# Output products that take tokens as weights in a test-time-training loop, and causal attention without its masked diagonal blocks

## The chip, the cores and the metric

The kernel runs on one core of a Trainium2 chip. The time is device microseconds of that core from start to end of one launch; a lower time is better. The times shown are medians of several executions, and beside them stands one execution that the hardware profiler recorded.

## The reference

Two transformer layers, each an attention-like part and a feed-forward part with adaptive layer norms, on a batch of 4 sequences of 512 tokens, 256 channels, in f32. The two parts that the change touches are the attention-like parts.

Layer 0 is a linear attention with fast weights. For each chunk of 64 tokens, with q, k, v per head (2 heads of 128 channels) and states w0, w1, w2 (128x128):

```python
gate = ki @ w0_; hb = ki @ w2_; hidden = silu(gate) * hb          # forward of keys
dhidden = vi @ w1_.transpose(0, 2, 1)                             # backward
w1g = newtonschulz5(einsum('bch,bcd->bhd', hidden * lr1i, vi))    # and w0g, w2g alike
w1_ = w1_ + w1g                                                   # then scaled to its first norm
o = (silu(qi @ w0_) * (qi @ w2_)) @ w1_                           # queries, then an RMS norm
```

Layer 1 is causal attention with 16 heads, 4 key groups, a latent of 64 channels for keys and values, and rotary positions on 64 channels. A query sees keys up to its own place, so in the last 128x128 square of each tile of queries the upper triangle is masked.

## The kernel before, in words

Everything is resident in SBUF; PSUM is eight banks of 128x512 f32. Each of the five engines runs its own program (TensorE, VectorE, ScalarE, GpSimd, and SyncE for the DMAs), in order, and they meet by counting semaphores. The order of the work is written out by hand.

**The loop over chunks** (`stage_fast_weights`). Eight steps (`NCH` = 8), each for all four sequences: a pair index `i` in 0 and 1, a half `j` of the partitions (64 tokens each), and a head `hd`, so eight (i, hd, j). Step 0 is written out, steps 1 to 5 are a hardware loop, steps 6 and 7 are written out, then comes `finish`. There are Q = 6 weight matrices of four units each: `3 * j + m`, m = 0, 1, 2 for w0, w2, w1. `state` holds them as they are updated and `weight` their transposes, which TensorE makes (`turn_weight`) and ScalarE or VectorE copies (`take_weight`).

A step on TensorE: `early_out` (the first of four calls of `out_product`, for the queries of the chunk before), `gates` (keys and values against the weights), two weight transposes, the second `out_product`, three groups of `gradient`, then `G_ORDER` (transposes GT of the gradients, column sums for their norms, and the third `out_product`, which stands there as `(OUT_ROWS, 0)`), then `INNER`, the Newton-Schulz products A, AA, Y, A1, AA1, YT, X2 for six matrices in a staggered order. Between these stand pieces of other work: the fourth `out_product` as `(OUT_ROWS, 1)`, `out_rows` (hidden against w1), `turn_out`, `project_out`, the turning of q, k, v of the next chunk, and `project_v` and `project_qk` of the one after it. At the step's end come `project_qk`, and four `turn_weight` as VectorE scales the states.

`out_product(m, j)` takes the weight as the stationary operand (128x128) and 64 tokens of `qT` as the moving one. Its result is transposed, channels on partitions: ScalarE takes the silu of bank 6 (`silu_out`, 128x512), and VectorE multiplies it with the other product (`hidden_out`, 128x512, after the third of the six A copies).

ScalarE, in a step: silu of q and k of the next chunk, weight copies, four activations for each pair of `gates`, gradient copies, `load_table(Sqrt)` and the root of the gradient norms (`g_norm`), copies of GT, AA, A1, YT, then the squares of states 4 and 5 (`SQUARED`), the roots of the weight norms (`root_state(1)`, then `root_state(0)` when VectorE's sums are there), `load_table(Silu)`, `take_proj`, weight copies 3 and 4. VectorE: squares of q and k, `backward`, squares of the gradients, the scaled copies (`scaled`), polynomials, updates of the state, `reduce_state` for states 3, 2, 0, 1, then `factors` and `scale_state`. GpSimd applies learning rates, moves q (`move_q`) and adds the output.

**The attention** (`stage_rest`). A batch is a tile of 128 queries of one row b of x: `ORDER` = (1, 3, 0, 2), 16 batches, with widths of 256, 512, 128 and 384 keys. A slot `t` is a batch and a pair of heads p (8 pairs): TensorE `score`, VectorE `largest` (the mask is added and the maximum taken in one instruction), ScalarE `exponential`, VectorE `invert`, GpSimd `normalize`, VectorE `turn` (transposes 32x32 blocks). `weigh(n - 1)` stands in slot 2 of batch n, all in one piece (the last batch has it in four pieces behind its slots). It multiplies blocks of 32 keys, in tiles of 32 rows by 64 columns: row group i holds queries 32i to 32i + 31, e is the head of the pair, and the moving operand is 8 pairs x 32 queries = 256 columns. `take_out` copies the result, `project_out` projects it. In the other slots stand the query projections of the next batch (`project_q`, "rope" in slots 0 and 1, "latent" in 4 and 5), and the values, keys and norms of the next row b. The feed-forward part of layer 0 lies between loop and attention, the routing and the experts of layer 1 behind them.

## Time and profile before

| what | value |
| --- | --- |
| median of three executions | 1028.23 us (1025.88 to 1028.37) |
| the profiled execution, its own time | 1024.87 us |
| span of the profile, first to last instruction | 1023.1 us |
| granted clock of TensorE over the span | 0.998 |
| busy: TensorE, VectorE, ScalarE, GpSimd | 970.8, 700.8, 564.5, 435.2 us |
| the loop, steps 1 to 7 | about 87 us to 360 us |
| the feed-forward part | about 362 us to 603 us |
| the attention's slots | 603 us to about 975 us |

Times in the profile are microseconds from its first instruction. PE is TensorE, PEld its weight loads, DVE is VectorE, ACT is ScalarE, POOL is GpSimd, SP is SyncE. Matmuls are pipelined and overlap, and a matmul's recorded duration is mostly latency: what a group costs is seen in the start of the next group. A f32 matmul has two records, a transpose one.

### The profile page before, as it was taken

How to read it: one execution, taken by the hardware profiler on the slowest of the kernel's cores; microseconds unless marked ns; L12 is line 12 of the kernel's file. 1: busy time of each engine (PE TensorE's matmuls, PEld its weight loads, DVE VectorE, ACT ScalarE, POOL GpSimd, SP SyncE). 2: the span in 40 equal slices, each digit the busy share in tenths (PEclk: the TensorE clock that was granted, in tenths of full speed). 3: DMA queues.
4: the chain of work that ended last, by engine and by line, in shares of the span. 5: the costliest groups of instructions: out<-in, count | busy, mean ns of one | idle time of the engine just before them, and what ended most of it. 6: DMA issues, size and time to landing. Idle time of an engine off the chain costs nothing.

```text
span 1023.1 us, 25038 instructions
## 1 busy us (share of the span) xinstructions
PE 970.8 (95%) x9714; PEld 738.6 (72%) x9714; DVE 700.8 (69%) x2121; ACT 564.5 (55%) x1450; POOL 435.2 (43%) x391
## 2 busy tenths in 40 slices
PE   5888999999999999999999999999999999999988
PEld 3566897888887755675656769786878687868646
DVE  4889988988989952213222676866787678766884
ACT  3668778777788742222223465565565556555541
POOL 1221140340542711101002666775677567779720
PEclk9999999999999999999999999999999999999999
DMA  9250000000000001900002321322132222211202
GB/s 313 70 196 2 2 0 0 0 0 0 0 2 2 1 1 36 322 1 0 1 1 53 83 62 44 72 59 57 43 74 53 58 48 66 60 42 44 93 3 84
DMA packets 32812, 52.36 MB, mean 51 GB/s; under 512 B 7760, under 2 KB 17744, under 8 KB 31824
## 3 DMA queue, kind: packets, MB, share of 16 engines
q1 hardware_dynamic: 32720, 51.10, 18.2%
q8 instruction: 62, 1.02, 0.4%
q14 instruction: 30, 0.25, 0.1%
HBM read 21.98 MB, written 2.10 MB: 24 GB/s over the span
## 4 chain that ended last, share of the span: by engine, by line
PE 53%; DVE 4%; ACT 2%; issue 1%
PE quad L2105 12%; PE quad L2064 10%; PE quad L1705 8%; PE quad L2122 7%; PE quad L2008 5%; PE quad L2136 5%; PE quad L2200 1%; PE quad L2072 1%; PE quad L1591 1%; ACT act_probs L2359 1%; ACT act_probs L2368 1%; PE quad L2027 1%; DVE act_probs L2460 1%; DVE wq_wo L2474 1%; DVE x_pairs L2490 0%
## 5 line engine op out<-in xcount | busy, mean ns | idle before, releaser
L2711 POOL TENSOR_TENSOR act_probs<-act_probs,rden 128x512 f32<-128x512 f32 (+3 forms) x128 | 169.1, 1327 | 110.6 <-DVE rden L2479 110.6
L2359 ACT ACTIVATE act_probs<-act_probs,neg_max 128x256 f32<-128x256 f32 (+3 forms) x256 | 141.0, 553 | 81.6 <-DVE neg_max L2460 81.4
L2064 PEld LDWEIGHTS quad<-hT,ug_queries 128*128 128x128 f32 x1024 | 122.6, 192 | 14.1 <-issue 7.7
L2064 PE MATMUL quad<-hT,ug_queries 128*128 128x128 f32 x1024 | 124.7, 275 | 0.8 <-DVE act_probs L1720 0.5
L2460 DVE CUSTOM_DVE_ANT_0 act_probs<-quad,mask 128x256 f32<-128x256 f32 (+3 forms) x256 | 115.0, 485 | 0.4 <-issue 0.3
L1705 PE MATMUL quad<-hT,ug_raw_switch 128*128 128x512 f32 x256 | 113.9, 595 | 0.0
L1720 DVE SCALAR_TENSOR_TENSOR act_probs<-quad,ws_up,silu_keys 128x512 f32<-128x512 f32 x32 | 24.0, 750 | 97.1 <-ACT silu_keys L1715 97.1
L1715 ACT ACTIVATE silu_keys<-quad,ws_gate 128x512 f32<-128x512 f32 x32 | 22.0, 688 | 118.6 <-PE quad L1705 118.6
L1705 PEld LDWEIGHTS quad<-hT,ug_raw_switch 128*128 128x128 f32 x256 | 47.4, 190 | 55.1 <-issue 54.3
L2479 DVE RECIPROCAL rden<-den 128x2 f32<-128x2 f32 x128 | 20.3, 159 | 94.6 <-ACT act_probs L2359 94.3
L2105 PE MATMUL quad<-down_raw_out,ug_raw_switch 128*128 128x256 f32 (+3 forms) x256 | 79.6, 438 | 3.2 <-DVE neg_max L2460 3.1
L2105 PE MATMUL quad<-silu_keys,ug_raw_switch 128*128 128x256 f32 (+3 forms) x256 | 79.7, 439 | 2.8 <-DVE neg_max L2460 2.0
L2474 DVE STREAM_TRANSPOSE wq_wo<-act_probs 128x1024 f32<-128x1024 f32 (+1 forms) x64 | 70.7, 1106 | 0.7 <-POOL act_probs L2711 0.4
L1426 POOL TENSOR_TENSOR hidden<-gate_silu,hb 128x256 f32<-128x256 f32 x16 | 12.0, 753 | 124.2 <-ACT hb L969 124.2
L2136 PE MATMUL quad<-down_keys,act_probs 128*128 128x256 f32 x256 | 60.5, 380 | 0.8 <-ACT act_probs L2368 0.8
L2105 PEld LDWEIGHTS quad<-down_raw_out,ug_raw_switch 128*128 128x128 f32 x256 | 42.4, 190 | 24.5 <-issue 15.2
L2105 PEld LDWEIGHTS quad<-silu_keys,ug_raw_switch 128*128 128x128 f32 x256 | 42.0, 190 | 24.9 <-issue 13.3
L2008 PE MATMUL quad<-down_raw_out,act_probs 128*128 128x256 f32 x256 | 56.1, 379 | 2.0 <-PEq L1510 2.0
L2136 PEld LDWEIGHTS quad<-down_keys,act_probs 128*128 128x128 f32 x256 | 47.9, 190 | 12.2 <-issue 2.9
L2008 PEld LDWEIGHTS quad<-down_raw_out,act_probs 128*128 128x128 f32 x256 | 48.3, 190 | 9.6 <-issue 3.3
L2122 PE MATMUL quad<-wq_wo,latent_rows 32*64 32x256 f32 x1792 | 51.5, 376 | 1.6 <-ACT gate L2345 0.8
L1206 DVE SCALAR_TENSOR_TENSOR q_bf<-quad,silu_keys 128x512 bf16<-128x512 f32 x72 | 46.3, 684 | 5.2 <-PE quad L645 5.0
(330 smaller groups left out, 2286.5 us busy)
## 6 DMA issues: line engine op xcount, KB each, us to landing
rope_swapped<-gate SPq DMA_DIRECT2D x120, 64.0 KB, 2.0
ug_raw_switch<-gate SPq DMA_DIRECT2D x60, 128.0 KB, 2.3
ug_raw_switch<-in_wmod SPq DMA_DIRECT2D x4, 512.0 KB, 7.1
x_pairs<-in_x SPq DMA_DIRECT2D x4, 512.0 KB, 7.6
x_rows<-x_pairs SPq DMA_DIRECT2D x8, 256.0 KB, 5.0
wq_wo<-in_wq_nopeT SPq DMA_DIRECT2D x1, 2048.0 KB, 8.5
wq_wo<-in_wo SPq DMA_DIRECT2D x1, 2048.0 KB, 13.0
ug_queries<-in_switch_w SPq DMA_DIRECT2D x1, 2048.0 KB, 7.7
```

Of the source, the lines that this page charges most:

```text
L1206: nc.vector.scalar_tensor_tensor(q_bf[:, q, :], bank[q][:], ca_b2, a_bf[:, q, :], ALU.mult, ALU.add).then_inc(taken[q], 1)
L1705: mm = k.nc.tensor.matmul(k.bank[2 * (m % 2) + w][:], self.w_ug[:, w, kt, P * m:P * m + P], k.hT[:, kt, 2 * i:2 * i + 2, 4 * C * u:4 * C * ...
L1720: k.nc.vector.scalar_tensor_tensor(self.act_t[:, m, :], k.bank[2 * (m % 2)][:], k.ws_up[:, m:m + 1], self.silu[:, m % 2, :], ALU.mult, ALU ...
L2008: mm = nc.tensor.matmul(bank[4 + q // 2][:, D * (q % 2):D * (q % 2) + D], act_t[:, m, P * q:P * q + P], w_down[:, ffn.place(m), :], start= ...
L2064: mm = nc.tensor.matmul(out[:, P * i:P * i + P], w[:, kt, HP * half + i, :], k.hT[:, kt, b, cols], start=(kt == 0), stop=(kt == KT - 1))
L2105: nc.tensor.matmul(score_bank[t % AHEAD][e][:, 0:width(n)], query[:, n % 2, e, p, :], keys[b % 2][:, p // 2, 0:width(n)], start=True, stop ...
L2122: mm = nc.tensor.matmul(av[LORA * e:LORA * e + LORA, i, :], val[rows, b % 2, j, :], src[rows, j, e, :, :], start=(j == 0), stop=(j == bloc ...
L2136: mm = nc.tensor.matmul(out[:, 0:D], oT[:, p, :], w_vo[:, p, :], start=(p == 0), stop=(p == NP - 1))
L2359: nc.scalar.activation(tile, tile, ACT.Exp, bias=neg_max[:, r, e:e + 1], scale=-1.0, accum_out=den[:, r, e:e + 1])\
L2460: nc.vector.tensor_tensor_reduce(probs[:, t % RING, e, 0:cols], score_bank[t % AHEAD][e][:, 0:cols], mask[:, L - cols:L], -QK_SCALE, 3e38, ...
L2474: nc.vector.transpose(turned_of[batches[n][1]][:, :, :, p, :].rearrange("p j e c -> p e j c"), probs[:, t % RING, :, 0:width(n)].rearrange ...
L2711: nc.gpsimd.tensor_tensor(tile, tile, rden[:, t % RING, :].unsqueeze(2).to_broadcast([P, 2, cols]), ALU.mult)\
```

## The change

The loop: `out_product` is used in `finish` alone. In its place `out_gate(t, i)` takes the tokens of q as the stationary operand (64 columns, on the column half j of the array) and both weights w0 and w2 as the moving one (256 columns), as `gates` does for k. Silu and product are done in halves (`silu_gate`, `hidden_rows`), tokens on partitions; then `turn_hidden` transposes the result with four f32 transposes, and ScalarE copies it (`take_hidden`). `early_out` goes; `gates` waits for the scaled states only ahead of its second part. At the step's end the second half of `project_qk` stands behind the last two `turn_weight`. State 3 is squared on ScalarE instead of VectorE from step 1 on (`SQUARED`), `take_proj` stands between the two roots, and the squares of q and k of the second pair stand at VectorE's start of the step. In step 7 GpSimd waits for a norm ahead of `move_q`.

The attention: for odd pairs p the queries of a tile are in reverse order, by a backward view of the moving operand in `project_q`. So in block d of the last four, row group i needs its even pairs only where d <= i and its odd pairs only where d <= 3 - i; `weigh` leaves the others out (`DIAGONAL`). The order in a block is row group outside (0, 3, 1, 2), head e inside. The mask and the rope tables have a backward half, `take_out` has an instruction for each parity and puts the order right.

Buffers: gate_pairs, hadamard and ws_dp share one tensor, in which the cosine table comes to lie after the loop; the cosine and sine tables are 512 KB each instead of 256, the mask has five squares instead of four.

In the diff below the table `TAKEN`, the buffers, `finish`, the rope tables and renamed semaphores are left out; context lines are dropped. `TAKEN` gets `(TURN_HID, 0)` ahead of `(AA, 0)`, for `take_hidden`; `out_rows` waits for it.

```diff
@@ -418,24 +419,24 @@
-    SQUARED = (4, 5)
+    SQUARED, SQUARED_FIRST = (4, 5, 3), (4, 5)
-    PROJECT_V, TURN_OUT, TURN_V, TURN_QK, OUT_ROWS, SUMS, START = range(PH, PH + 7)
-    G_ORDER = ((GT, 0), (SUMS, 0), (OUT_ROWS, 0), (SUMS, 1), (SUMS, 2), (GT, 2), (SUMS, 3), (SUMS, 4), (GT, 4), (SUMS, 5))
+    PROJECT_V, TURN_OUT, TURN_V, TURN_QK, OUT_ROWS, SUMS, START, OUT_GATE, TURN_HID = range(PH, PH + 9)
+    G_ORDER = ((GT, 0), (SUMS, 0), (OUT_GATE, 1), (SUMS, 1), (SUMS, 2), (GT, 2), (SUMS, 3), (SUMS, 4), (GT, 4), (SUMS, 5))
-    INNER = ((A, 0), (A, 1), (OUT_ROWS, 1), (START, 0), (A, 2), (A, 3), (AA, 0), (A, 4), (AA, 1), (START, 1), (A, 5), (TURN_V, 0), (AA, 2), (OUT_ROWS, 0), (START, 2), (AA, 3), (Y, 0), (AA, 4), (AA, 5), (START, 3), (TURN_QK, 0), (Y, 1),
+    INNER = ((A, 0), (A, 1), (TURN_HID, 0), (START, 0), (A, 2), (A, 3), (AA, 0), (A, 4), (AA, 1), (START, 1), (A, 5), (TURN_V, 0), (AA, 2), (OUT_ROWS, 0), (START, 2), (AA, 3), (Y, 0), (AA, 4), (AA, 5), (START, 3), (TURN_QK, 0), (Y, 1),
-    NORM_QK, HIDDEN, MEAN_OUT, NORM_OUT = 1, 2, 0, 0
+    NORM_QK, MEAN_OUT, NORM_OUT = 1, 0, 0
...
@@ -560,12 +561,33 @@
+                    if i == 0 and (isinstance(t, bass.RuntimeValue) or t > 0):
+                        pe.wait_ge(s["w_scaled"], Q * t)
+            def out_gate(t, i):
+                if i == 0:
+                    pe.wait_ge(s["proj_taken"], t)
+                    pe.wait_ge(s["q_moved"], t)
+                else:
+                    pe.wait_ge(s["out_hidden"], 2 * t - 1)
+                for hd in range(H):
+                    for j in range(2):
+                        mm = nc.tensor.matmul(bank[6][C * j:C * j + C, 2 * HD * hd:2 * HD * hd + 2 * HD],
+                                              qT[:, i, hd, C * j:C * j + C], weight[:, 3 * j:3 * j + 2, H * i + hd, :],
+                                              start=True, stop=True)
+                mm.then_inc(s["out_summed"], 1)
+            def turn_hidden(t):
+                pe.wait_ge(s["out_hidden"], 2 * t)
+                for u in range(U):
+                    mm = nc.tensor.transpose(bank[6][:, P * u:P * u + P], h_o[:, P * u:P * u + P], k.eye[:])
+                mm.then_inc(s["o_turned"], 1)
...
@@ -577,7 +599,10 @@
-                pe.wait_ge(s["out_hidden"], c + 1)
+                if at == 6:
+                    pe.wait_ge(s["hid_taken"], c + 1)
+                else:
+                    pe.wait_ge(s["out_hidden"], 2 * NCH - 1)
...
@@ -647,8 +666,6 @@
-                if not first:
-                    early_out(t)
                 pe.wait_ge(s["qkv_taken"], 3 * (t + 1))
...
@@ -656,7 +673,6 @@
                         begin(q, G)
-                    pe.wait_ge(s["w_scaled"], Q * t)
                 gates(t)
...
@@ -668,8 +684,7 @@
                     turn_weight(t - 1, 2)
-                    begin(0, G)
-                    out_product(0, 0, 0)
+                    out_gate(t, 0)
...
@@ -714,9 +729,7 @@
                     else:
-                        if n == 0:
-                            pe.wait_ge(s["out_silued"], t)
-                        out_product(1, n)
+                        out_gate(t, n)
                 pe.wait_ge(s["g_columns_taken"], t + 1)
...
@@ -741,11 +754,10 @@
+                    elif ph == TURN_HID and not first:
+                        turn_hidden(t)
-                        if n == 1:
-                            out_product(1, 1)
-                        else:
-                            out_rows(t - 1)
+                        out_rows(t - 1)
...
@@ -795,10 +807,10 @@
+                    turn_weight(t, 0)
+                    turn_weight(t, 1)
-                    turn_weight(t, 0)
-                    turn_weight(t, 1)
...
@@ -915,6 +927,15 @@
+            def silu_gate(t, i):
+                act.wait_ge(s["out_summed"], 2 * (t - 1) + i + 1)
+                nc.scalar.activation(h_o[:, H * P * i:H * P * i + H * P].rearrange("p (h d) -> p h d", h=H),
+                                     bank[6][:].rearrange("p (h g d) -> p h g d", h=H, g=2)[:, :, 0, :], ACT.Silu).then_inc(s["out_silued"], 1)
+            def take_hidden(t):
+                act.wait_ge(s["o_turned"], 2 * t - 1)
+                nc.scalar.activation(hid_o[:].rearrange("p i h c -> p (i h c)"), bank[6][:], ACT.Copy).then_inc(s["hid_taken"], 1)
...
@@ -979,10 +999,12 @@
-                    silu_out(t - 1)
+                    silu_gate(t, 0)
+                if not first:
+                    silu_gate(t, 1)
...
@@ -1040,22 +1064,23 @@
-                        act.wait_ge(s["w_squared"], 2 * t + 2)
-                    act.wait_ge(s["w_reduced"], 4 * t + 4 - 3 * j)
+                        act.wait_ge(s["w_squared"], 3 * t + 2)
+                    if first or j == 0:
+                        act.wait_ge(s["w_reduced"], 1 if j == 1 else 3 * t + 4)
-                for q in SQUARED:
+                for q in SQUARED_FIRST if first else SQUARED:
+                if first:
+                    nc.scalar.activation(add[:, 0, 0:1], k.neg_half[:, 0:1], ACT.Copy).then_inc(s["proj_taken"], 1)
+                else:
+                    take_proj(t - 1)
-                if first:
-                    nc.scalar.activation(add[:, 0, 0:1], k.neg_half[:, 0:1], ACT.Copy).then_inc(s["proj_taken"], 1)
-                else:
-                    take_proj(t - 1)
...
@@ -1128,8 +1153,14 @@
-            def hidden_out(c, at=6):
-                dve.wait_ge(s["out_silued"], c + 1)
+            def hidden_rows(t, i):
+                dve.wait_ge(s["out_silued"], 2 * (t - 1) + i + 1)
+                to = h_o[:, H * P * i:H * P * i + H * P].rearrange("p (h d) -> p h d", h=H)
+                nc.vector.tensor_tensor(to, bank[6][:].rearrange("p (h g d) -> p h g d", h=H, g=2)[:, :, 1, :], to, ALU.mult)\
+                    .then_inc(s["out_hidden"], 1)
+            def hidden_out(c, at):
+                dve.wait_ge(s["out_silued"], 2 * NCH - 1)
...
@@ -1177,6 +1208,8 @@
+                if not first:
+                    hidden_rows(t, 0)
...
@@ -1209,6 +1242,8 @@
+                    dve.wait_ge(s["qkv_acted"], 3 * (t + 1) + 2)
+                    square_qk(t + 1, 1, (0, 1, 2, 3))
...
@@ -1228,12 +1263,13 @@
-                if more:
-                    dve.wait_ge(s["qkv_acted"], 3 * (t + 1) + 2)
-                    square_qk(t + 1, 1, (0, 1, 2, 3))
-                    if first:
-                        mods.guard_gates(dve, 0)
-                else:
+                if not first:
+                    hidden_rows(t, 1)
+                if first:
+                    dve.wait_ge(s["qkv_acted"], 5)
+                    square_qk(1, 1, (0, 1, 2, 3))
+                    mods.guard_gates(dve, 0)
+                elif not more:
...
@@ -1251,8 +1287,6 @@
-                    if not first and n == HIDDEN:
-                        hidden_out(t - 1)
...
@@ -1305,7 +1339,7 @@
-                    if n == 3:
+                    if first and n == 3:
...
@@ -1433,6 +1467,7 @@
+                    pool.wait_ge(norms.xn_done, norms.groups[LN0B].end)
...
@@ -1835,6 +1870,10 @@
+    EVERY, FORWARD, BACKWARD = slice(0, NP), slice(0, NP, 2), slice(1, NP, 2)
+    DIAGONAL = [[(i, EVERY if d <= min(i, ROWS - 1 - i) else FORWARD if d <= i else BACKWARD)
+                 for i in (0, 3, 1, 2) if d <= max(i, ROWS - 1 - i)] for d in range(ROWS)]
+    LAST_OF = [max(i, ROWS - 1 - i) for i in range(ROWS)]
...
@@ -1961,6 +2000,13 @@
+    def in_order(tokens, p):
+        return tokens[:, ::-1] if p % 2 else tokens
+    def mask_of(n, p):
+        q = batches[n][1]
+        return mask[:, q::-1, :] if p % 2 else mask[:, QT - q:QT + 1, :]
...
@@ -2061,7 +2107,7 @@
-                        mm = nc.tensor.matmul(out[:, P * i:P * i + P], w[:, kt, HP * half + i, :], k.hT[:, kt, b, cols],
+                        mm = nc.tensor.matmul(out[:, P * i:P * i + P], w[:, kt, HP * half + i, :], in_order(k.hT[:, kt, b, cols], i),
...
@@ -2116,11 +2162,13 @@
-                    for e in range(2):
-                        for i in range(ROWS):
-                            rows = slice(BLK * i, BLK * i + BLK)
-                            mm = nc.tensor.matmul(av[LORA * e:LORA * e + LORA, i, :], val[rows, b % 2, j, :], src[rows, j, e, :, :],
-                                                  start=(j == 0), stop=(j == blocks - 1))
+                    d = max(0, j - (blocks - ROWS))
+                    for i, pairs in DIAGONAL[d]:
+                        rows = slice(BLK * i, BLK * i + BLK)
+                        for e in range(2):
+                            out = av[LORA * e:LORA * e + LORA, i, :].rearrange("p (n c) -> p n c", c=BLK)
+                            mm = nc.tensor.matmul(out[:, pairs, :], val[rows, b % 2, j, :], src[rows, j, e, pairs, :],
+                                                  start=(j == 0), stop=(d == LAST_OF[i]))
...
@@ -2364,8 +2412,9 @@
-                for heads in [slice(0, NP)] if n < NB - 1 else [slice(0, HP), slice(HP, NP)]:
-                    nc.scalar.activation(to[:, heads], src[:, heads], ACT.Copy).then_inc(s["oT_taken"], 1)
+                for lo, hi in [(0, NP)] if n < NB - 1 else [(0, HP), (HP, NP)]:
+                    nc.scalar.activation(to[:, lo:hi:2], src[:, lo:hi:2], ACT.Copy)
+                    nc.scalar.activation(to[:, lo + 1:hi:2, ::-1, ::-1], src[:, lo + 1:hi:2], ACT.Copy).then_inc(s["oT_taken"], 1)
...
@@ -2457,8 +2506,9 @@
-                    nc.vector.tensor_tensor_reduce(probs[:, t % RING, e, 0:cols], score_bank[t % AHEAD][e][:, 0:cols],
-                                                   mask[:, L - cols:L], -QK_SCALE, 3e38, ALU.add, ALU.min,
+                    nc.vector.tensor_tensor_reduce(probs[:, t % RING, e, 0:cols].rearrange("p (w c) -> p w c", c=P),
+                                                   score_bank[t % AHEAD][e][:, 0:cols].rearrange("p (w c) -> p w c", c=P),
+                                                   mask_of(*divmod(t, NP)), -QK_SCALE, 3e38, ALU.add, ALU.min,
```

## Rows read from the trace of the kernel before

**Rows 1.** The page: busy time by engine, and the chain that ended last.
```profile
PE 970.8 (95%) x9714; PEld 738.6 (72%) x9714; DVE 700.8 (69%) x2121; ACT 564.5 (55%) x1450; POOL 435.2 (43%) x391
...
PE 53%; DVE 4%; ACT 2%; issue 1%
```

**Rows 2.** One loop step by windows: its length, busy time per engine, clock.
```profile
166.26:205.50 39.24, 38.52 (x472) 32.92 (x471) 35.34 (x115) 30.79 (x83) 10.57 (x14) 1.00 0.00 0
```

**Rows 3.** TensorE's timeline in that step: start, length, operation, records.
```profile
166.26 1.08 PE L559 MATMUL quad<-weight,kT 128*64 128x256 f32 x8
167.17 0.61 PE L565 MATMUL quad<-state,vT 128*64 128x128 f32 x8
...
178.25 1.06 PE L574 MATMUL quad<-qT,weight 128*128 128x64 f32 x8
179.14 0.61 PE L645 MATMUL quad<-act_probs 128*128 128x128 bf16 x8
...
191.85 0.61 PE L592 MATMUL quad<-eye,o_n 128*128 128x128 f32 x4
192.30 0.39 PE L645 MATMUL quad<-silu_keys 128*128 128x128 bf16 x4
...
201.52 1.26 PE L618 MATMUL quad<-eye,state 128*128 128x128 f32 x8
202.62 1.02 PE L537 MATMUL quad<-w_qkv,h_chunk 128*128 128x512 f32 x2
203.48 1.04 PE L618 MATMUL quad<-eye,state 128*128 128x128 f32 x8
204.45 1.10 PE L574 MATMUL quad<-qT,weight 128*128 128x64 f32 x8
205.50 1.08 PE L559 MATMUL quad<-weight,kT 128*64 128x256 f32 x8
```

**Rows 4.** ScalarE's timeline at the end of that step.
```profile
200.43 0.21 ACT L1045 ACTIVATE w_n<-w_rows 128x12 f32<-128x12 f32 x1 [2.07 <-DVE w_rows L1287]
...
202.54 1.08 ACT L937 ACTIVATE weight<-quad 128x512 f32<-128x512 f32 x2
```

**Rows 5.** VectorE's timeline in that step.
```profile
167.92 0.43 DVE L1158 TENSOR_TENSOR d_hb<-quad,gate_silu 128x256 f32<-128x256 f32 x1 [1.36 <-PE quad L565]
...
180.17 0.68 DVE L1134 TENSOR_TENSOR out_hidden<-quad,out_silu 128x512 f32<-128x512 f32 x1
...
200.78 1.29 DVE L1303 TENSOR_TENSOR state<-state,w_f 128x512 f32<-128x512 f32 x2
...
202.45 2.50 DVE L1303 TENSOR_TENSOR state<-state,w_f 128x512 f32<-128x512 f32 x4
```

**Rows 6.** Groups by line, 60 to 300 us: count | busy us, mean ns.
```profile
L1287 DVE CUSTOM_DVE_ANT_0 act_probs<-state 128x128 f32<-128x128 f32 x96 | 21.3, 288 | 0.0
...
L1036 ACT ACTIVATE act_probs<-state 128x128 f32<-128x128 f32 x48 | 14.0, 297 | 0.0
```

**Rows 7.** TensorE's timeline in the attention, batches 2 and 3.
```profile
626.01 7.17 PE L2122 MATMUL quad<-wq_wo,latent_rows 32*64 32x256 f32 x256 [0.29 <-issue]
633.10 1.16 PE L2105 MATMUL quad<-silu_keys,ug_raw_switch 128*128 128x128 f32 x8
...
664.97 1.10 PE L2105 MATMUL quad<-down_raw_out,ug_raw_switch 128*128 128x256 f32 x4 [0.88 <-DVE neg_max L2460]
```

**Rows 8.** VectorE's timeline ahead of that wait.
```profile
662.59 1.75 DVE L2490 TENSOR_TENSOR x_pairs<-x_pairs,rope_sin 128x512 f32<-128x512 f32 x1
```

**Rows 9.** Groups by line, whole span, TensorE.
```profile
L2064 PE MATMUL quad<-hT,ug_queries 128*128 128x128 f32 x1024 | 124.7, 275 | 0.8 <-DVE act_probs L1720 0.5
...
L2159 PE MATMUL quad<-hT,ug_raw_switch 32*32 32x384 f32 x128 | 4.5, 493 | 1.4 <-DVE attn_gated L2500 1.0 <-DVE ug_raw_switch L2554 0.3
...
L2170 PE MATMUL quad<-hT,ug_raw_switch 32*32 32x128 f32 x128 | 2.5, 277 | 0.9 <-issue 0.9
```

59 lines of the change are left out of this document (31 added, 28 removed).

## The prediction

> **What bounds the kernel now.** I read the page first, then the waits and the timelines of one loop step, then those of the attention. TensorE is busy for 95% of the span, and most of the chain that ended last is its own work [rows 1]; in the loop its granted clock is 1.00, the 2.4 GHz level [rows 2]. So a step is worth what it takes from TensorE's stream, if no other engine is late instead.
>
> The first place of the change is the loop over the eight chunks. A step lasts 39.24 us, TensorE busy for 38.52, VectorE for 35.34 and ScalarE for 30.79 [rows 2]. The reader should use the start times in TensorE's timeline, not the durations, since matmuls overlap: a group costs the distance to the next group's start. One f32 matmul shows as two records. A call of `out_product` (eight records, 128x128 weights, 64 moving columns) costs 0.89 us (178.25 to 179.14) among the A products, and 1.05 us at the step's start with the wait behind it (204.45 to 205.50). The same number of records with 64 columns of weights and 256 moving columns costs 0.91 us (166.26 to 167.17), though each moves four times the columns [rows 3]. So the former cost is not that of its columns. Four f32 transposes cost 0.45 us (191.85 to 192.30) [rows 3].
>
> The second place is the weighing of the values in the attention, in 32x64 tiles: 16 key blocks take 7.09 us, 626.01 to 633.10 [rows 7], so 0.443 us for a block of sixteen records, or 27.7 ns a record. TensorE is there bound by its own stream too, but not everywhere: at 664.97 it has waited 0.88 us for VectorE [rows 7], which is at work on the keys of the next batch, 1.75 us in one instruction [rows 8].
>
> **The loop, part by part.** (1) Four calls of `out_product` go, and two of `out_gate` come, each built like one half of `gates`: 0.91 us each. Two of them stand where `out_product` stood (ahead of the gradients, and in `G_ORDER`), so some 0.9 becomes 0.91 twice; I count nothing. The other two places lose their product: 1.05 at the step's start and 0.89 among the A products. `turn_hidden` adds 0.45. TensorE's stream is 1.05 + 0.89 - 0.45 = 1.49 us shorter per step.
>
> (2) What replaces the cover at the step's start. The early product hid ScalarE's copies of weights 0 and 1. Now the second part of `project_qk`, 0.86 us (202.62 to 203.48, [rows 3]), moves behind the last two transposes and covers them. Those transposes can now come earlier than VectorE's scaled state 0: VectorE scales two states from 200.78 and four from 202.45 [rows 5], and the transposes of weight 3 start at 201.52 [rows 3]. VectorE itself comes earlier, because `reduce_state(3)` leaves it: four squares at 21.3/96 = 0.22 us [rows 6], 0.9 us. The last updates then wait for TensorE's last products instead, so perhaps 0.4 of the 0.9 are gained beyond the shift of the whole step. That is enough for weight 3, while weight 0 is a little late: I leave 0.15 us for a new wait there.
>
> (3) ScalarE gets state 3, four squares at 14.0/48 = 0.29 us [rows 6], their reads overlapping: 1.2 us more. It had idled 2.07 us before the second root [rows 4], and VectorE needs that root only after its own remaining three reductions. `take_proj` moves into that idle time as well, which pulls the first weight copy (202.54, [rows 4]) some 0.5 us forward. I count nothing here, the idle time being longer than the squares; the upper bound is that the third square gives 0.8 us per step back.
>
> (4) The hidden product in halves. VectorE has one product over 512 columns, 0.68 us at 180.17, in the middle of its scaled copies [rows 5]. It becomes two over 256, about 0.43 each (as the row at 167.92, [rows 5]): one in idle time behind `backward`, one behind the column sums. The A copies are thus 0.6 us closer together, which matches the product that TensorE loses there, so that TensorE's gain can be realised. ScalarE's half `silu_gate` now stands ahead of the table load for the root of the gradient norms; it delays that root by 0.15 us, of which VectorE feels 0.05, as its squares behind the column sums go. Queued behind that root are the root of the q and k norms and the five copies of GT, for which the A products wait. Its `take_hidden` lies behind the last GT copy, where ScalarE waits for TensorE anyway.
>
> (5) The squares of q and k for the second pair move to the step's start, 0.84 us, ahead of `backward`. VectorE waits there 1.36 us for `gates` [rows 5]: they fit, with 0.05 us to spare. Both bounds: nothing, or 0.4 us per step if the second silu comes late, since the whole backward pass is queued behind them.
>
> Sum: 1.49 - 0.15 - 0.05 = 1.29 us a step. Seven steps (1 to 7) have the products: 9.0 us. Bounds: 7 x 1.49 = 10.4, and 7 x (1.29 - 0.8) = 3.4.
>
> **The attention.** (6) Of the last four key blocks of each tile of queries, the masked parts go. Odd head pairs hold their tokens backward, so every row group streams 640 columns of 1024: 256, 256 or 128, 128, and 128 for two row groups alone. Four blocks take 4 x 0.443 = 1.77 us now, and at best 640/1024 of that, 1.11: a saving of 0.66. Issue is strictly in order, and a short tile waits behind a long one at two places; that and the cost of short records take some back. 128 records of 384 columns in 32x32 tiles cost 4.5 us and of 128 columns 2.5 us: 35 and 20 ns [rows 9]. There sixteen tiles run side by side, here eight, so 128 columns less are worth the same 15 ns a record here, if no floor stands in the way, and the floor may be as high as those 20. I take 16 ns, between 27.7 - 15 and 20. Then 24 full records at 27.7, 24 short ones at 16 and the eight of the last block, which have half of the tiles, at 27 make 1.26 us: 0.5 us saved. Bounds 0.66, and 0.2 for the floor and a loss at each change of width.
>
> (7) That happens 16 times. At the third batch of each of the first three rows of x the gain ends in the wait for VectorE of [rows 7]; so it does at the very end, where VectorE's routing is the longer branch, and half of it in the last batch. 11.5 x 0.5 = 5.8 us; bounds 11.5 x 0.2 = 2.3 and 16 x 0.66 = 10.6.
>
> (8) Costed at nothing: `take_out` in two instructions instead of one (about 0.1 us of ScalarE, ahead of an output product four slots later; without that cover 0.1 us x 16); the mask and the rope tables as views of more dimensions (same element counts); tables of twice the size, which land while TensorE runs the feed-forward part; the shared buffer, whose first users are done by then. In step 7 GpSimd now waits for `normalize` of VectorE ahead of `move_q`; behind it stands only an `add_out`, and TensorE needs the moved q in `finish`, a projection and eight transposes later.
>
> (9) The one operation with no near row: half of the query projection now reads its moving operand backward. The rows have 1024 records of it, all forward, 124.7 us or 0.12 us each [rows 9]. Bounds: nothing, or a doubled stream for 512 records, 62 us. I take nothing, as the nearest row: 256 columns taken in two pieces far apart run at full rate in `gates` [rows 3]. 
>
> **Sum.** 9.0 + 5.8 = 14.8 us off the profiled execution of 1024.9 us: 1010.1. The median of the runs shown is 3.4 us above that execution, so 1013.5.
>
> **Rivals.**
> A (forecast), both parts gain: 1013.5, own range 1008 to 1019; chance 0.64.
> B, the loop gives most of it back. VectorE and ScalarE have more to do in the same stretches, and the second `silu` or the third square ends last. For it: VectorE's 35.34 of 39.24 us, and margins of 0.05. Against: its own work falls by 0.6. 3.4 + 5.8 = 9.2: 1019; chance 0.12.
> C, the attention gives nothing: short records cost as much as long ones, or VectorE and GpSimd, not TensorE, set the slots. For it: [rows 8]. Against: TensorE's stream is unbroken in most batches. 9.0: 1019; chance 0.12. B and C together: 1025; 0.03.
> D, slower: the backward read. It decides from 14.8 us / 512 = 29 ns a record, a quarter over today's distance. At the doubled rate 1013.5 + 62 = 1075; chance 0.06.
> E, slower: tiles in the same rows don't overlap. The order in a block becomes row group outside, column half inside. Where the second half had to wait for the first, the 96 whole blocks would go from 0.44 to 0.89 us and the 16 diagonals from 1.26 to 2.2: some 58 us more, 1071. `gates` speaks against it: its column halves share all rows, and 256 columns pass in 0.91/8 = 0.114 us [rows 3], no more than 128 columns in the query projection, which has the whole array (0.12, [rows 9]); so the halves do run side by side. The Trainium skill ("TensorE: Matmul & The Clock Gate", the mechanism of row and column tiling) says that a weight load overlaps with running matmuls only where the row group differs; by that rule E would hold, and by the row A does. Chance 0.03.
>
> **How the numbers follow.** A measurement here tells 0.3%, 3 us, from no change. Faster by more: A, B, C, and half of both together: 0.64 + 0.24 + 0.02 = 0.90, less 0.02 for runs that scatter by 2.5 us: 0.88. Same: 0.03. Slower: 0.09. The range reaches from A's low end to B and C: 1007 to 1021 holds some 0.82.
>
> **What would show it.** TensorE's timeline: no 64-column product at the start of a step, `gates` directly behind the 512-column projection, step length near 38 us; `out_gate` at 0.91 us. ScalarE's idle time before the second root gone, VectorE's 1.36 us before `backward` gone. In the attention: the four last blocks of a tile in 1.2 to 1.3 us, the query projection at 0.12 us a record in both directions, the stall of [rows 7] longer by about 0.5. I am wrong if a step stays over 38.5 us, if the projection's records lengthen, or if the waits for VectorE in the attention grow by as much as the weighing shrinks.

## The result and the profile after

The changed kernel takes 1016.8 us (median of 4 runs, 1013.95 to 1018.83), the kernel before 1027.1 in the runs beside it: a ratio of 0.9898, 95% interval 0.9876 to 0.9919. A later pairing gave 0.9896 (0.9879 to 0.9913). The forecast was 1013.5, range 1007 to 1021, faster.

The page of the changed kernel, busy times first, then the chain (compare [rows 1]):

```profile
PE 954.8 (94%) x9502; PEld 718.5 (71%) x9502; DVE 695.5 (69%) x2072; ACT 576.7 (57%) x1537; POOL 435.5 (43%) x391
...
PE 46%; DVE 8%; ACT 2%; issue 2%; POOL 1%; DMA 0%; SPq 0%; DVEq 0%; POOLq 0%
```

One loop step of it by windows, from the first `gates` record of step 3 to that of step 4, as in [rows 2] (columns: length, busy time of PE, PEld, DVE, ACT, POOL, granted clock, DMA share, GB/s):

```profile
166.75:205.05 38.30, 37.45 (x460) 30.60 (x459) 34.75 (x106) 32.36 (x92) 10.57 (x14) 1.00 0.00 0
```

The step has lost 0.94 us, not 1.29. TensorE's timeline of that step, the lines that answer to [rows 3]:

```profile
163.25 1.04 PE L643 MATMUL quad<-eye,state 128*128 128x128 f32 x8
164.70 1.26 PE L643 MATMUL quad<-eye,state 128*128 128x128 f32 x8 [0.41 <-DVE state L1337]
165.79 1.02 PE L538 MATMUL quad<-w_qkv,h_chunk 128*128 128x512 f32 x2
166.75 1.08 PE L560 MATMUL quad<-weight,kT 128*64 128x256 f32 x8
...
170.52 1.08 PE L581 MATMUL quad<-weight,qT 128*64 128x256 f32 x8
171.53 0.72 PE L632 MATMUL quad<-d_hb,k_lr 64*128 64x128 f32 x8
...
174.82 1.08 PE L581 MATMUL quad<-weight,qT 128*64 128x256 f32 x8
175.84 0.35 PE L720 MATMUL quad<-ones_bf,q_bf 128*128 128x1 bf16 x8
...
178.81 0.61 PE L589 MATMUL quad<-eye,out_silu 128*128 128x128 f32 x4
179.25 0.69 PE L664 MATMUL quad<-act_probs 128*128 128x128 bf16 x8
```

The reader is to see three things. `gates` (L560) stands directly behind the projection part (L538), as forecast. An `out_gate` (L581) costs 1.01 and 1.02 us to the next group's start, where 0.91 was forecast. The transposes of weight 0 (164.70) wait 0.41 us for VectorE, where 0.15 was.

In the attention, TensorE's timeline of the second weighing and of the wait in the third batch ([rows 7]), and the query projection by line ([rows 9]):

```profile
621.96 6.52 PE L2170 MATMUL quad<-wq_wo,latent_rows 32*64 32x256 f32 x248 [0.29 <-issue]
628.41 1.16 PE L2151 MATMUL quad<-silu_keys,ug_raw_switch 128*128 128x128 f32 x8
...
660.35 1.10 PE L2151 MATMUL quad<-down_raw_out,ug_raw_switch 128*128 128x256 f32 x4 [1.48 <-DVE neg_max L2509]
```

```profile
L2110 PE MATMUL quad<-hT,ug_queries 128*128 128x128 f32 x1024 | 124.7, 275 | 1.2 <-ACT act_probs L2417 0.5 <-DVE act_probs L1755 0.5
```

Sixteen key blocks take 6.45 us (621.96 to 628.41) instead of 7.09: 0.64 less, where 0.5 was forecast. The wait for VectorE has grown from 0.88 to 1.48 us: in that batch nearly all of the gain ends in it. The projection with half of its tokens backward costs the same 124.7 us.

**Where the time came from.** Milestones of TensorE, in us between first records (the start is counted from 0.13 us of the profile), in the profiled executions:

| stretch | before | changed | changed, second profile |
|---|---|---|---|
| start to gates(0) | 31.92 | 33.53 | 32.99 |
| steps 0 and 1 | 94.97 | 94.79 | 94.80 |
| steps 2 to 6 | 195.86 | 191.14 | 191.10 |
| step 7 to the feed-forward part | 35.27 | 36.21 | 36.20 |
| feed-forward part | 190.97 | 189.57 | 191.26 |
| to the first weighing | 54.71 | 55.04 | 55.06 |
| first to last weighing | 372.88 | 365.49 | 368.57 |
| last weighing to last product | 42.66 | 42.30 | 42.30 |

So the loop gives 4.0 us, nothing of it in steps 0 and 1, and 1.4 more at the head of the feed-forward part, where TensorE had waited for VectorE's last state; 5.4 in all where 9.0 were forecast. TensorE's timeline there, before and changed:

```profile
361.72 1.28 PE L618 MATMUL quad<-eye,state 128*128 128x128 f32 x8
363.43 0.63 PE L618 MATMUL quad<-eye,state 128*128 128x128 f32 x4 [0.44 <-issue]
365.07 0.66 PE L618 MATMUL quad<-eye,state 128*128 128x128 f32 x4 [1.01 <-DVE state L1303]
365.56 2.74 PE L1705 MATMUL quad<-hT,ug_raw_switch 128*128 128x512 f32 x6
```

```profile
359.23 1.04 PE L643 MATMUL quad<-eye,state 128*128 128x128 f32 x8
360.75 1.21 PE L643 MATMUL quad<-eye,state 128*128 128x128 f32 x8 [0.48 <-issue]
361.79 3.60 PE L1740 MATMUL quad<-hT,ug_raw_switch 128*128 128x512 f32 x8
```

VectorE's timeline shows why the last state was late: three of its last four scalings of a state before, and all four in the changed kernel.

```profile
362.64 4.06 DVE L1303 TENSOR_TENSOR state<-state,w_f 128x512 f32<-128x512 f32 x3
```

```profile
359.95 2.50 DVE L1337 TENSOR_TENSOR state<-state,w_f 128x512 f32<-128x512 f32 x4
```

Before, GpSimd runs its two instructions on the output from 362.91 and 364.54 us (1.54 and 1.61 us), and the two scalings beside them take 1.76 us each instead of 0.69. In the changed kernel GpSimd's two start at 356.19 and 358.02 us, end ahead of the last four scalings, and slow one of the first two. `attn_only` has the late meeting and `loop_only` hasn't. The nearest cause is `take_proj`, which now stands ahead of ScalarE's second root and so gives GpSimd its operand earlier; no run moves it alone.

The attention gives 7.4 + 0.4 where 5.8 were forecast. That makes 13.2 us; the start, 1.6 us later, and 0.3 ahead of the first weighing leave the 11.2 between the two spans. The second profile of the changed kernel loses 1.7 us in the feed-forward part and 3.1 in the attention to falls of the granted clock and waits that the first doesn't have (last section).

### The profile page after: what moved, and what is told of

It is laid out like the page before. It is cut to its first block, busy times and chain, and to the rows that moved or that the text cites. A ratio compares the mean times of both kernels' runs of the same rounds, so it can differ in the third digit from the quotient of the medians.

```text
span 1011.9 us, 24653 instructions
## 1 busy us (share of the span) xinstructions
PE 954.8 (94%) x9502; PEld 718.5 (71%) x9502; DVE 695.5 (69%) x2072; ACT 576.7 (57%) x1537; POOL 435.5 (43%) x391
## 4 chain that ended last, share of the span: by engine, by line
PE 46%; DVE 8%; ACT 2%; issue 2%; POOL 1%; DMA 0%; SPq 0%; DVEq 0%; POOLq 0%
PE quad L2151 9%; PE quad L1740 8%; PE quad L2110 8%; PE quad L2054 5%; PE quad L2170 5%; PE quad L2184 4%; DVE act_probs L2509 2%; DVE wq_wo L2524 2%; PE quad L2248 1%; DVE x_pairs L2541 1%; ACT act_probs L2407 1%; PE quad L2118 1%; PE quad L1626 1%; PE quad L2073 1%; ACT hT L1639 1%
## 5 line engine op out<-in xcount | busy, mean ns | idle before, releaser
L2110 PE MATMUL quad<-hT,ug_queries 128*128 128x128 f32 x1024 | 124.7, 275 | 1.2 <-ACT act_probs L2417 0.5
L2509 DVE CUSTOM_DVE_ANT_0 act_probs<-quad,mask 128x128 f32<-128x128 f32 (+3 forms) x160 | 65.3, 445 | 0.0
L2509 DVE CUSTOM_DVE_ANT_1 act_probs<-quad,mask 128x256 f32<-128x256 f32 (+2 forms) x96 | 49.4, 551 | 0.0
```

Source lines behind the costliest of these rows:

```text
L2110: mm = nc.tensor.matmul(out[:, P * i:P * i + P], w[:, kt, HP * half + i, :], in_order(k.hT[:, kt, b, cols], i), start=(kt == 0), stop=(kt ...
L2509: nc.vector.tensor_tensor_reduce(probs[:, t % RING, e, 0:cols].rearrange("p (w c) -> p w c", c=P), score_bank[t % AHEAD][e][:, 0:cols].rea ...
```

## The experiments

A step length in the trace repeats to 0.02 us between kernels with the same loop, a whole execution only to some us (the changed kernel's four lie between 1013.95 and 1018.83); so small edits are judged by the trace.

**One part alone.** `loop_only` leaves the attention as before, `attn_only` the loop.

> The loop's part of the change alone; the attention is as before. Theory, the two parts are independent: a steady step lasts 38.3 us as in the changed kernel (39.24 before), the feed-forward part ends some 3.8 us earlier than before, and the attention's weighings last as before (5.1 and 6.8 us for 12 and 16 key blocks). Time about 3 to 4 us under before, ratio 0.9965. Rival, the loop's gain of 0.94 us in a step reaches the end in full (6 x 0.94 = 5.6 us and more), and what was missing in the profile of the changed kernel (a start 1.6 us later, at a granted clock of 0.50 in 20 to 22 us) was an accident of that one execution: then the start is at 31.9 us here and the time 5 to 6 us under before.

> The attention's part of the change alone, with the reversed order of tokens of odd head pairs, and the shared buffer; the loop is as before. Theory, the parts are independent: step 39.24 us, each of 16 weighings 0.52 us shorter, first to last weighing 365.5 us as in the changed kernel (372.9 before), time about 7 us under before, ratio 0.993. Rival, with the loop as before the tables of twice the size land while nothing else changed, and the first batch waits for them: then the ratio is nearer 1 and the gap shows before the first weighing. The first steps of the program: the granted clock in 20 to 22 us is 1.00 if its fall in the changed kernel was an accident of one execution, 0.50 if the kernel brings it.

Measured: `loop_only` 1023.2 us, ratio 0.9964 (0.9949 to 0.9978); `attn_only` 1020.9, 0.9949 (0.9932 to 0.9965). The two ratios together make 8.9 us of gain, against 10.5 by the ratio of the whole change: the parts add up within the intervals. Steps 2 to 4 are 38.28 to 38.29 us in the first, 39.22 to 39.24 in the second; from first gates to feed-forward part 322.05 and 325.84 (326.11 before, 322.14 changed). The loop's gain up to there is 4 us, so the first theory holds; steps 0 and 1 give nothing (94.79 in the first, 94.72 in the second). The feed-forward part is 190.98 us in the second, as before, so its 1.4 us are the loop change's too. In `loop_only` a fall of the granted clock takes them back there (191.27). From its first to its last weighing it has 373.98 us, against 372.88 before; these two are why 5.4 us of the trace are 3.7 in the times, as far as one profile can tell. `attn_only` falls short of the 7 us expected: 5.2, with 366.75 us from first to last weighing instead of 365.5. Starts are at 33.22 and 33.15 us without a fall of the clock: the early start of the profile before (31.92) was no property of it (31.35 to 33.53 in all profiles).

**Nothing left out.** `reversed_whole`: the changed kernel, with

```
-    DIAGONAL = [[(i, EVERY if d <= min(i, ROWS - 1 - i) else FORWARD ...
-    LAST_OF = [max(i, ROWS - 1 - i) for i in range(ROWS)]
+    DIAGONAL = [[(i, EVERY) for i in (0, 3, 1, 2)] for d in range(ROWS)]
+    LAST_OF = [ROWS - 1] * ROWS
```

> The changed kernel, but every weighing goes over all key blocks of all pairs again, with the reversed tokens and with the new order of tiles (row group outside, column half inside); the masked parts add zeros. Theory, the backward read and the new order cost nothing and all of the attention's gain is the columns left out: weighings last 5.1 and 6.8 us as before, the query projection 0.12 us a record, time that of the loop change alone (7 us over the changed kernel). Rival, the new order has a part in the gain or in a loss: weighings of whole blocks differ from 0.443 us a block; 0.02 us a block would be 3 us in the time.

Measured: 1023.8 us, 0.9977 (0.9966 to 0.9988), beside 0.9964 for `loop_only`. From first to last record the weighings of 4, 8 and 12 blocks last 1.61, 3.34 and 5.07 us, as before. The four of 16 blocks spread from 6.86 to 8.25 (`loop_only`: 6.79 to 7.41). So backward reads and the new order of tiles are free as far as this can tell; what makes the weighings of 16 blocks scatter wasn't followed. Their two intervals overlap, and 1 us between them is not decided.

**Left out in the plain way.** `triangle`, on top of `loop_only`:

```
                 for j in range(lo, hi):
-                    for e in range(2):
-                        for i in range(ROWS):
+                    d = max(0, j - (blocks - ROWS))
+                    for i in range(d, ROWS):
+                        for e in range(2):
```

> The loop change, and an attention that leaves the masked parts out in the plain way: tokens forward for all pairs, and key block d of the last four goes only to the row groups from d on, 10 of 16 pairs of row group and block, each record at full width. Theory, what a weighing costs is the stream of its fullest row group: the last row group still streams all four blocks, so nothing is saved: weighings within 0.1 us of before, time that of the loop change alone. Rival, what it costs is records issued: 12 of 32 records of the last four blocks go, 27.7 ns each (0.443 us for 16): 12 x 0.0277 = 0.33 us less a weighing, 5 us less in all; if four blocks shrink by the share of records, 0.66 us, 10 us in all.

(A matmul here is two records, so the rival's price should have read 24 of 64 records: 0.66 us by either count.) Measured: 1021.9 us, 0.9954 (0.9941 to 0.9968). TensorE's timeline of the second weighing:

```profile
623.37 7.17 PE L2157 MATMUL quad<-wq_wo,latent_rows 32*64 32x256 f32 x232 [0.29 <-issue]
630.47 0.71 PE L2139 MATMUL quad<-silu_keys,ug_raw_switch 128*128 128x128 f32 x4
```

232 records instead of 256 take 7.10 us, as before. Shown: what a weighing costs is the stream of the row group with the most columns. It is not the number of records, and not the sum of the columns either, which is 640 of 1024 of the last four blocks both here and in the changed kernel. The reversal of odd pairs is what makes the omission pay, since it brings every row group to 640 of 1024 columns; and 1.77 x 384/1024 = 0.66 is what it paid (0.64).

**The third square on VectorE again**, and **the cover back** ahead of the transposes 0 and 1:

```
-    SQUARED, SQUARED_FIRST = (4, 5, 3), (4, 5)
+    SQUARED, SQUARED_FIRST = (4, 5), (4, 5)
...
-                    if first and n == 3:
+                    if n == 3:
                         reduce_state(3)
```

```
+                    if ahead:
+                        project_qk(t + 2, 1, [1])
                     turn_weight(t, 0)
                     turn_weight(t, 1)
-                    if ahead:
-                        project_qk(t + 2, 1, [1])
```

> The changed kernel with the squares of state 3 back on VectorE, behind the fourth update, in steps 1 to 7 too. Judged by the length of the steps of 38.30 us, from gates to gates. Theory, VectorE's chain of updates, sums, factors and scalings sets the end of the step now: the transposes of weight 0 already wait 0.41 us for its state 0, so its four sums, 0.9 us, come on top: 39.1 to 39.2 us, and that wait grows to about 1.3. The move of the squares is then what makes the loop's change a gain at all. Rival, the forecast's upper bound: the squares cost ScalarE as much as they give VectorE, and the step changes by less than 0.2 us either way.

> The changed kernel with the last part of the query and key projection (0.96 us) again ahead of the transposes of weights 0 and 1. Judged by the steps of 38.30 us. Theory: the wait of 0.41 us for state 0 goes, but the part no longer covers ScalarE's two copies of the weights, 0.6 us each, for which gates waits: steps 38.5 to 38.6 us. Rival, the wait for state 0 is a pure loss and the copies are early enough: steps 37.9 us.

Measured by steps 2 to 4: 38.68 to 38.69 and 38.35 to 38.36 us, against 38.30. Having VectorE's squares of state 3 on ScalarE is worth 0.39 us a step, not 0.9. TensorE's wait for state 0 didn't grow as expected (0.42 us); all of VectorE's end of the step comes later. In the changed kernel VectorE waits 0.24 us for TensorE ahead of its last update (158.66), so part of the 0.9 had gone into waiting there; the rest wasn't followed. It is worth 0.75 in step 6 (37.89 to 38.64), which has no projection to put ahead, and about 1.2 at the head of the feed-forward part (192.48 with a fall of the clock, 191.26 in the changed kernel with one). Moving the cover is worth nearly nothing (0.05). In `cover_back` the wait of 0.41 us for VectorE's state 0 is gone, and `gates` waits 0.79 us for ScalarE's copy of a weight instead.

**out_gate in the same shape of tiles.** `same_mode`:

```
                 gates(t)
+                if not first:
+                    out_gate(t, 0)
...
                     turn_weight(t - 1, 5)
                     turn_weight(t - 1, 2)
-                    out_gate(t, 0)
```

ScalarE's `silu_gate` and copy of weight 2 change places for it, and VectorE's copy of weight 5 comes later.

> The changed kernel with the first out_gate directly behind gates, whose tile shape it shares, and the transposes of weights 5 and 2 behind it; ScalarE and VectorE take those weights correspondingly later. Judged by the steps of 38.30 us. Theory, an out_gate costs 1.02 us and not the forecast's 0.91, and its neighbours up to 0.1 more, because TensorE drains where the shape of its tiles changes from 128x128 to 128x64 and back; one change to and one from it less are worth 0.15 to 0.2 us: 38.1 to 38.15. Rival, the 1.02 is the reading of qT or the wait for a bank, and the place is nothing: 38.3. Second rival, the later copies of weights 5 and 2 hold up the gradients: 38.5 or more.

Measured: 38.14 to 38.15 us, 0.15 less. From the first record of `gates` to that of the gradients it is 4.64 us instead of 4.78, with no wait in either, so the changes of tile shape (128 x 128 to 128 x 64 and back) around one `out_gate` are what is left to cost that. But steps 0 and 1 took 96.75 us together instead of 94.5 to 95.2 in the kernels with the changed loop and no fall of the clock there. Step 0, whose code is untouched, took 55.87 of them (54.2 to 55.4 in the others), at a granted clock of 0.80 and 0.78 in 50 to 54 and 54 to 58 us.

**Step 1.** VectorE's and TensorE's timelines of the changed kernel at the start of step 1:

```profile
86.99 0.19 DVE L395 TENSOR_SCALAR out_hidden<-out_hidden 128x72 f32<-128x72 f32 x1
...
89.65 0.49 DVE L1393 TENSOR_SCALAR w_proj<-w_proj,onorm 128x512 f32<-128x512 f32 x1
...
91.57 0.81 DVE L1136 CUSTOM_DVE_ANT_0 act_probs<-qkv 128x128 f32<-128x128 f32 x1
...
92.95 0.41 DVE L1189 TENSOR_TENSOR d_hb<-quad,gate_silu 128x256 f32<-128x256 f32 x1
```

```profile
92.02 1.08 PE L581 MATMUL quad<-weight,qT 128*64 128x256 f32 x8
94.94 1.16 PE L632 MATMUL quad<-d_hb,k_lr 64*128 64x128 f32 x16 [1.84 <-DVE d_gate_out L1191]
```

Here VectorE has 3.2 us of work on the learning rates and the projection's weights ahead of its step (86.99 to 90.19), and the idle time into which the squares were moved doesn't exist. The gradients wait 1.84 us (0.21 before). Two kernels, with VectorE's step 1 taken out of its loop:

```
late_in_step_1, in step 1 alone:     room_in_step_1, in step 1 alone:
 square_qk(t + 1, 0, ...)             backward(t, first)
-square_qk(t + 1, 1, ...)            +w_proj scaled, ffn.scale_signs(dve)
 backward(t, first)                   (both were ahead of step 1)
 ...
 hidden_rows(t, 1)
+square_qk(t + 1, 1, ...)
```

> The changed kernel with VectorE's squares of the second pair of q and k at their former place, behind the column sums, in step 1 alone. Judged by gates(1) to gates(2), 40.21 us in the changed kernel and 39.79 before. Theory: in step 1 VectorE comes late, with 3.2 us of work on the learning rates ahead of its step, so the squares moved ahead of the backward pass, 0.84 us and more, lie on the path, where TensorE's gradients wait 1.84 us for it (0.21 before): step 1 takes 38.8 to 39.3 us, and the wait falls under 0.9. Rival, the wait of 1.84 us is the backward pass itself on late weights: step 1 stays above 40 us.

> The changed kernel, with VectorE's scaling of the projection weights and of the signs (0.65 us) in step 1 behind the backward pass, where VectorE waits for TensorE's gradients anyway. Theory: VectorE's work between the scaling of the states and the backward pass is what the gradients of step 1 wait for; their wait of 1.84 us falls to about 1.2, and with work taken out of the path and not only moved along it, it stays gained: gates(0) to gates(2) 94.1 us, against 94.8. Rival: it is given back in the same step, and 94.5 us or more come out.

Measured: the wait fell to 1.43 and 1.57 us (it is 1.84 and 2.24 in the changed kernel's own two profiles), and steps 0 and 1 together took 94.50 and 94.55 us, against 94.79. Both theories fall in their size, and the numbers of both rivals came: step 1 of `late_in_step_1` stays above 40 us (40.34), and `room_in_step_1` is above 94.5. Of the later squares 0.3 us stay. TensorE's timeline of `late_in_step_1` shows one place where the rest went:

```profile
101.34 0.40 PE L664 MATMUL quad<-act_probs 128*128 128x128 bf16 x4 [0.61 <-ACT act_probs L972]
```

ScalarE's copies of GT stand behind `root_qk`, which waits for these squares. Of the 0.65 us moved out of the way 0.25 stay; what takes the rest was not followed.

**The changed kernel again, and three edits joined.** `best` is `same_mode` with the edit of `room_in_step_1`, and in step 7 two of `normalize`'s four instructions behind the fourth scaled copy of A. In step 7 VectorE does `normalize` (1.37 us) ahead of g_norm, which the later half product now delays. TensorE's timeline there in the changed kernel:

```profile
331.99 0.70 PE L664 MATMUL quad<-act_probs 128*128 128x128 bf16 x8
333.37 0.23 PE L664 MATMUL quad<-silu_keys 128*128 128x128 bf16 x1 [0.68 <-DVE silu_keys L1234]
```

> The changed kernel as it is, once more, beside the next one on the same chip, and for a second trace of it. Theory: the loop from the first gates to the first product of the feed-forward part lasts 322.1 us again, steps 38.30, since these repeated to 0.1 us in three other kernels with the same loop; the ratio to before is 0.989 to 0.991. The start, which was 31.4 to 33.5 us in ten profiles with no relation to the kernel, and the feed-forward part (189.6 to 192.5) may differ by 1 to 2 us. Rival: the fall of the granted clock to 0.50 at 20 to 22 us belongs to the changed kernel; then it comes again, and the start is 33.5.

> The changed kernel with three edits: the first out_gate directly behind gates (0.15 us a step); in step 1 VectorE's scaling of the projection weights and of the signs behind the backward pass instead of ahead of the step (0.65 us); in step 7 two of the four normalizations behind the fourth scaled copy of A, so that g_norm is not kept waiting (0.3 to 0.7 us, the wait of 0.68 of TensorE). Theory: loop from first gates to the feed-forward part 320.0 to 320.6 us, against 322.1, and a time 1.5 to 2 us below the changed kernel's on the same chip. Rival: VectorE is late again at the next place in each of the two steps (as in step 1 with the later squares, where 0.42 us gained were lost 5 us on), so that only the 6 x 0.15 us stay: 321.2.

Measured: the changed kernel 1016.85 us, with the loop as expected (322.09) and no fall of the clock at the start, so that one belongs to an execution and not to the kernel. `best` 1017.6 us, 0.9912 (0.9896 to 0.9929): not better. Step 7 did gain 1.0 us up to the feed-forward part (35.19), and then TensorE waited 2.66 us. VectorE's, TensorE's and GpSimd's timelines in `best`, and windows:

```profile
350.94 1.38 DVE L1328 CUSTOM_DVE_ANT_0 act_probs<-state 128x128 f32<-128x128 f32 x1
...
352.24 2.43 DVE L1328 CUSTOM_DVE_ANT_0 act_probs<-state 128x128 f32<-128x128 f32 x1
...
356.09 1.34 DVE L1328 CUSTOM_DVE_ANT_0 act_probs<-state 128x128 f32<-128x128 f32 x1
...
357.57 0.28 DVE L1328 CUSTOM_DVE_ANT_0 act_probs<-state 128x128 f32<-128x128 f32 x1
```

```profile
353.58 3.60 PE L1745 MATMUL quad<-hT,ug_raw_switch 128*128 128x512 f32 x8
359.84 3.59 PE L643 MATMUL quad<-eye,state 128*128 128x128 f32 x16 [2.66 <-DVE state L1344]
```

```profile
352.13 2.40 POOL L1515 TENSOR_TENSOR gate<-gate,gate_pairs 128x1024 f32<-128x1024 f32 x1
354.49 1.31 POOL L1448 TENSOR_TENSOR proj_gated<-proj_gated,gate_pairs 128x512 f32<-128x512 f32 x1
```

```profile
358.00:360.00 2.00, 0.16 (x1) 0.16 (x2) 1.93 (x12) 1.24 (x2) 0.00 (x0) 0.95 0.00 0
360.00:362.00 2.00, 2.00 (x10) 1.88 (x11) 1.93 (x6) 1.99 (x6) 0.00 (x0) 0.50 0.00 0
```

A square that takes 0.28 us alone took up to 2.43 beside GpSimd's products, as if it stood still until one of them was done: the one from 352.24 ends at 354.67, and GpSimd's from 352.13 at 354.53. GpSimd came 1.8 us later by the time of the profile, and 3.0 us later against `gates(7)`, because it waits for the fourth `normalize`. `best2` puts two of the four right behind the backward pass, and two back in their place (against the changed kernel):

```
                 backward(t, first)
+                if not more:
+                    norms.normalize(dve, LN0B, 0, 2)
...
-                    norms.normalize(dve, LN0B)
+                    norms.normalize(dve, LN0B, 2, 4)
```

> The edits of the kernel called best, but in step 7 two of the four normalizations stand right behind the backward pass and two at their old place, so that they are done no later than before. What undid best: GpSimd waits for the fourth normalization ahead of move_q; it came 1.8 us later, its queue then ran beside VectorE's squares of the states, each of which took 0.97 to 2.43 us instead of 0.28, and TensorE waited 2.66 us for state 3, at a granted clock of 0.50 afterwards. Theory: with GpSimd in time again, the squares take 0.28 us (the first one 0.5), TensorE does not wait for state 3, gates(7) to the feed-forward part lasts 35.3 to 35.6 us, steps 38.15; the time is 1 to 2 us below the changed kernel's 1016.85, if step 0 keeps its clock, and equal if it loses 1.4 us to it again as in the two kernels with out_gate moved. Rival: GpSimd's stream overlaps the squares here too, and TensorE waits again.

Measured: 1013.6 us (1011.38 to 1013.82), ratio 0.9860 (0.9841 to 0.9880), 3.3 us below the changed kernel. Steps 38.14 to 38.15, steps 0 and 1 94.61, step 7 35.39, loop 320.38 us; the same squares in `best2`:

```profile
349.27 0.56 DVE L1328 CUSTOM_DVE_ANT_0 act_probs<-state 128x128 f32<-128x128 f32 x1
...
349.77 0.28 DVE L1328 CUSTOM_DVE_ANT_0 act_probs<-state 128x128 f32<-128x128 f32 x1
```

No wait for state 3, and no fall of the clock in 50 to 58 us, where `same_mode` and `best` had one. By the trace 1.8 us of loop are won (322.14 to 320.38); the other 1.5 are within the spread of whole executions. The intervals of the two ratios just touch (0.9880 and 0.9879).

## Why the forecast held, point by point

The time lay 3.3 us over the forecast, inside A's own range (1008 to 1019). That it lay so near is in part luck, since two errors partly cancel: the loop gave 5.4 us instead of 9.0, the attention 7.8 instead of 5.8. By the traces that makes 13.2 of the forecast 14.8; that the medians show 10.3 I put down to the falls of the clock, of which the profile before has only the one at the end of step 0, but that is argued from few profiles.

- **(1) Mis-sized.** "Two of them stand where `out_product` stood, I count nothing": the two places cost 0.17 us more each (the gradients are 0.16 later against `gates`, and the step 0.34 later behind the second). `out_product` runs in the shape of tiles of its neighbours, `out_gate` doesn't. `same_mode` shows 0.15 of it.
- **(2) Mis-sized.** The start of the step lost 0.65 us instead of 1.05 - 0.15: the wait for state 0 is 0.41, not 0.15. (Two small terms cancel in it: the projection records ahead of the transposes of weight 3 take 2.57 us instead of 2.74, and the groups behind them 0.16 us more.) VectorE's sums stand in the way, and moving the squares of state 3 to ScalarE gives 0.39 of the 0.9 (`third_square_dve`). The mechanism was right: without the move four tenths of the step's gain go. Where the cover stands doesn't matter (`cover_back`).
- **(3)** Right in the steady steps: ScalarE's idle time ahead of the second root is gone and nothing waits for it. In step 7 VectorE waits 0.55 us for ScalarE's first root (355.66).
- **(4)** Better than forecast. Up to the A products the step stood 0.34 us later; a wait of some 0.27 among the first A products, which stood ahead of `out_product`, went too, and the hidden product's removal gave 0.46 less 0.09. Sum of the step: +0.34 - 0.64 - 0.65, with rounding the measured 0.94.
- **(5)** Right in steps 2 to 6, where VectorE's 1.36 us ahead of `backward` are gone and no gradient waits. (The margin of 0.05 us isn't what 1.36 and 0.84 leave, 0.52; in the trace the second pair's silu comes 0.19 us late, and `backward` still starts 1.66 us after `gates`, as before.) It failed as a claim on seven steps. I read one steady step and multiplied by 7. Step 1 gained nothing, and step 7 lost 0.93 where it was to gain: there `normalize` stands where the squares stand in the others, and the A products wait for g_norm. Instead of 7 x 1.29 it was 4.7 in steps 2 to 6, 0.2 in steps 0 and 1, less 0.9 in step 7, and 1.4 behind it, of which I had counted nothing: the meeting of VectorE and GpSimd that the earlier `take_proj` ends.
- **(6) Mis-sized**, 0.64 instead of 0.5 a weighing. The floor for short records, which I took from 32x32 tiles ([rows 9]), isn't met: short records cost their columns.
- **(7)** Right. Between the starts of weighings the changed kernel is 0.62, 0.54, 0.03 and 0.86 us shorter in the first four batches, and 0.63, 0.54, 0.03 and 0.64 in the next four: the third gives nothing, as forecast.
- **(8)** The step-7 wait of GpSimd was costed at nothing, which holds as long as `normalize` stays where it is; `best` shows what it costs otherwise.
- **(9)** Right: 0.12 us a record in both directions. The Trainium skill's note ("SBUF — State Buffer", cachelines), that successive reads within a line run at full bandwidth, agrees with these 124.7 us.

**Rivals.** B priced the loop at 3.4 and A at 9.0; it gave 5.4. B's mechanism held in steps 1 and 7, and not in a steady step. C is refuted by `attn_only` (5.2 us), and `triangle` beside the changed kernel shows that the columns of the fullest row group are what counts. D is refuted by the 124.7 us. E is refuted by `reversed_whole`: with the halves of a row group in succession the weighings last as before. The Trainium skill ("TensorE: Matmul & The Clock Gate", the mechanism of row and column tiling) says that a weight load overlaps with running matmuls only where the row group differs. By that rule the prediction had them doubled; here the measurement decides against it for f32 in column halves.

What stays open: what takes the 0.4 us given back in `room_in_step_1`, whether the reversed whole tiles cost the 1 us by which `reversed_whole` lies over `loop_only`, and how the 0.9 us lost in step 7 divide between the later g_norm and the rest.

## What to carry to other kernels

- A loop that is peeled at its ends has to be read at its ends: multiply a steady step's gain only by the steps that have its slack.
- Where work is left out of tiles that run side by side, only the fullest tile's stream counts; balance first, then leave out.
- A small move on one engine is also a move of everything that waits for it on another. Look whose stream it now runs beside.
